# A four-layer block on one core: attention scores from fp16 halves, query and key biases as a product, projections and one value projection in other steps

## What is computed

```python
q = (x @ Wq + bq).reshape(B, S, N_HEAD, HEAD_DIM).transpose(0, 2, 1, 3)
k = (x @ Wk + bk).reshape(B, S, N_HEAD, HEAD_DIM).transpose(0, 2, 1, 3)
v = (x @ Wv + bv).reshape(B, S, N_HEAD, HEAD_DIM).transpose(0, 2, 1, 3)
scores = jnp.einsum('bhqd,bhkd->bhqk', q / math.sqrt(HEAD_DIM), k)
scores = scores + attention_bias
scores = jnp.where(src_mask, -jnp.inf, scores.astype(jnp.float32))
probs = jax.nn.softmax(scores, axis=-1).astype(v.dtype)
ctx = jnp.einsum('bhqk,bhkd->bhqd', probs, v)
```

## Time and profile before

| | |
|---|---|
| median of 3 runs | 2546.38 us (2546.37 to 2546.72) |
| the profiled execution, its own time | 2548.05 us |
| its span, first to last instruction | 2546.2 us |
| PE, DVE, ACT, POOL busy, share of the span | 97%, 75%, 44%, 38% |
| attention pass | to about 1082 us, eight sequences |

### The profile page before, as it was taken

The page is one execution under the profiler, slowest core; times in us unless marked ns, Lnnn a source line. Parts: engine busy times, 40 slices in busy tenths (PEclk is TensorE's granted clock), DMA queues, the critical chain, the costliest instruction groups (busy, mean ns, idle before and its releaser), DMA issues.

```text
span 2546.2 us, 45850 instructions
## 1 busy us (share of the span) xinstructions
PE 2470.9 (97%) x14369; PEld 1223.5 (48%) x14456; DVE 1921.7 (75%) x3700; ACT 1127.6 (44%) x2160; POOL 978.1 (38%) x829
## 2 busy tenths in 40 slices
PE   6999999999999999999999999999999999999996
PEld 4454545455555555544444444444444444444443
DVE  7877777777778685663598688678786886886887
ACT  3676757575758575742223223233222322232331
POOL 1464646464646464410044143242341441432321
PEclk8999999999999999999999999999999999999998
DMA  6445444454544445551232142133222321421340
GB/s 221 143 152 162 150 154 160 147 166 148 158 148 156 150 150 168 163 191 42 79 112 90 61 141 89 56 120 115 83 87 91 108 91 62 141 84 58 123 169 17
DMA packets 150760, 312.29 MB, mean 123 GB/s; under 512 B 16642, under 2 KB 21762, under 8 KB 150546
## 3 DMA queue, kind: packets, MB, share of 16 engines
q1 hardware_dynamic: 141330, 293.01, 35.1%
q10 hardware_dynamic: 9216, 16.78, 1.8%
HBM read 292.75 MB, written 16.81 MB: 122 GB/s over the span
## 4 chain that ended last, share of the span: by engine, by line
PE 53%; DVE 3%; issue 1%; ACT 0%; DVEq 0%; ACTq 0%
PE ffn_bank L1469 17%; PE ffn_bank L1471 17%; PE ffn_bank L1470 17%; PE ffn_bank L1455 1%; PE ffn_bank L1533 1%; PE ffn_bank L1475 1%; DVE g2T_hi L1777 1%; DVE g2T_lo L1778 0%; DVE w_lo L1835 0%; DVE w_hi L1835 0%; PE ffn_bank L1566 0%; DVE stage L1740 0%; ACT g L1611 0%; DVE stage L1721 0%; DVE f L1829 0%
## 5 line engine op out<-in xcount | busy, mean ns | idle before, releaser
L1077 DVE CUSTOM_DVE_ANT_0 w_words<-bank,stage 128x512 f32<-128x512 f32 x512 | 323.7, 686 | 92.7 <-PE bank L688 86.7
L857 ACT ACTIVATE w_words<-w_words,nmax 128x512 f32<-128x512 f32 x512 | 363.4, 714 | 42.2 <-DVE nmax L1077 42.1
L561 POOL TENSOR_TENSOR stage<-stage,mask_add 128x1024 f32<-128x1024 f32 x128 | 272.9, 2143 | 215.3 <-DMA stage<-in_bias 197.6
L1777 DVE CAST g2T_hi<-g 128x512 f16<-128x512 f32 x256 | 179.5, 701 | 221.0 <-ACT g L1611 216.5
L711 PE MATMUL bank<-ident,w_words 128*128 128x128 f32 x2048 | 299.6, 280 | 16.2 <-DVE late L1092 4.7
L711 PEld LDWEIGHTS bank<-ident,w_words 128*128 128x128 f32 x2048 | 222.7, 140 | 175.2 <-issue 83.4
L1778 DVE TENSOR_TENSOR g2T_lo<-g,g2T_hi 128x512 f16<-128x512 f32 x256 | 243.6, 951 | 8.8
L1611 ACT ACTIVATE g<-ffn_bank,bi 128x512 f32<-128x512 f32 x128 | 88.0, 687 | 350.1 <-PE ffn_bank L1471 328.9
L843 ACT ACTIVATE late<-bank 128x512 f32<-128x512 f32 x256 | 151.0, 590 | 151.7 <-PE bank L711 151.5
L1405 POOL TENSOR_TENSOR late<-late,b 128x512 f32<-128x512 f32 x32 | 39.6, 1269 | 464.0 <-DVE f L1809 464.0
L1391 POOL TENSOR_TENSOR stage<-grid,f 128x512 f32<-128x512 f32 x84 | 138.5, 1675 | 200.2 <-DVE f L1680 75.3
(11 more groups left out here) (277 smaller groups left out, 4886.3 us busy)
## 6 DMA issues: line engine op xcount, KB each, us to landing
stage<-in_bias SPq DMA_DIRECT2D x256, 512.0 KB, 4.3
stage<-in_W_l SPq DMA_DIRECT2D x128, 512.0 KB, 3.3
grid<-in_grids SPq DMA_DIRECT2D x140, 256.0 KB, 3.6
xin<-in_x SPq DMA_DIRECT2D x32, 256.0 KB, 4.0
x_rows<-w_words ACTq DMA_DIRECT2D x32, 256.0 KB, 3.7
late<-x_rows SPq DMA_DIRECT2D x8, 1024.0 KB, 8.7
out<-stage ACTq DMA_DIRECT2D x32, 256.0 KB, 2.0
l_rows<-in_rows SPq DMA_DIRECT2D x8, 768.0 KB, 6.6
```

The source lines that it names most:

```text
L561: pool.tensor_tensor(bias[:, n % NB, :, :], bias[:, n % NB, :, :], mask_add[:, u % T, :].unsqueeze(1).to_broadcast([P, 2, S]), ALU.add).th ...
L857: act.activation(tile, tile, ACT.Exp, scale=-1.0, bias=nmax[:, u % 2, i:i + 1], accum_out=rsum[:, j, h:h + 1]).then_inc(prob_ready, 1)
L1077: dve.tensor_tensor_reduce(tiles[:, 4 * (u % NR) + i, :], bank[:, :], bias[:, half % NB, i % 2, :], -1.0, 3.0e38, ALU.add, ALU.min, nmax[: ...
L1777: link(dve.tensor_copy(gT[0][:, n % 4, :], g32[:, n % 2, :]))
```

## The change

- `q32` and `k32` become pairs of fp16 halves. ScalarE writes the high half of both `q` and `k` (activation Copy with the scale), VectorE then the low half of both (the bank times the scale, minus the high half). Before, each was one instruction of one engine.
- The scores of four heads are three rounds of four fp16 products (high by high, high by low, low by high) where there were four fp32 products.
- The biases of q and k are no longer added on the way out. GpSimdE prepares once, before the loop, a tile of two rows (high and low half of the scaled bias), and every `q` or `k` projection ends with one more product of these two rows with a tile of ones.
- The table: `v 3` moves from step 1 to step 3; `q 1`, `k 1` from steps 2, 3 to 1, 2; `q 2`, `k 2` from 6, 7 to 5, 6; `q 3`, `k 3` from 10, 11 to 9, 10. The first product with v waits for each value tile alone.

```diff
-BESIDE = {0: [("v", 2), ("xT", 0), ("xT", 1)], 1: [("v", 3), ("xT", 2), ("xT", 3)],
-          2: [("down",), ("q", 1)], 3: [("expert",), ("k", 1)], 4: [("up", 0), ("up", 1)],
-          5: [("R", 0), ("up", 2), ("up", 3)], 6: [("q", 2)], 7: [("k", 2)], 9: [("R", 1)], 10: [("q", 3)],
-          11: [("k", 3)], 13: [("R", 2)], 17: [("R", 3)]}
+BESIDE = {0: [("v", 2), ("xT", 0), ("xT", 1)], 1: [("xT", 2), ("xT", 3), ("q", 1)],
+          2: [("down",), ("k", 1)], 3: [("expert",), ("v", 3)], 4: [("up", 0), ("up", 1)],
+          5: [("R", 0), ("up", 2), ("up", 3), ("q", 2)], 6: [("k", 2)], 9: [("R", 1), ("q", 3)], 10: [("k", 3)],
+          13: [("R", 2)], 17: [("R", 3)]}
...
+            pool.tensor_scalar(b_scaled, b_raw, WS, None, ALU.mult).then_inc(b_chain, 1)
...
+            pool.memset(ones[:, :], 1.0).then_inc(b_chain, 1)
...
-                        mm = three(bank[:, :], w, x, c == 0, c == C - 1)
+                        mm = three(bank[:, :], w, x, c == 0, c == C - 1 and name == "v")
+                    if name != "v":
+                        if m == 0:
+                            pe.wait_ge(b_chain, 7)
+                        mm = pe.matmul(bank[:, :], qk_b[:, "qk".index(name), m * P:(m + 1) * P], ones[:, :].to_broadcast([2, S]), start=False, stop=True)
...
-                    for i in range(4):
-                        rows = slice(HD * i, HD * i + HD)
-                        pe.matmul(psum[i][:, :], q32[rows, g, j * P:(j + 1) * P], k32[rows, g, :],
-                                  start=i < 2, stop=True).then_inc(full[i], 1)
+                    for n, (qs, ks) in enumerate(((0, 0), (0, 1), (1, 0))):
+                        for i in range(4):
+                            rows = slice(HD * i, HD * i + HD)
+                            mm = pe.matmul(psum[i][:, :], q16[qs][rows, g, j * P:(j + 1) * P], k16[ks][rows, g, :],
+                                           start=n == 0 and i < 2, stop=n == 2)
+                            if n == 2:
+                                mm.then_inc(full[i], 1)
...
-                        pe.wait_ge(v32_ready, 1 + it * T + T)
+                    if v == 0:
+                        pe.wait_ge(v32_ready, 1 + it * T + kb + 1)
...
-                        act.activation(q32[:, m, :], bank[:, :], ACT.Identity, scale=1.0 / (WS * math.sqrt(HD)),
-                                       bias=bq[:, m:m + 1]).then_inc(q32_ready, 1)
+                        act.activation(q16[0][:, m, :], bank[:, :], ACT.Copy, scale=Q_SCALE).then_inc(q_hi, 1)
+                    elif name == "k":
+                        bank = arrived(act, it, key)
+                        act.activation(k16[0][:, m, :], bank[:, :], ACT.Copy, scale=1.0 / WS).then_inc(k_hi, 1)
...
-                            for key in beside(it, u):
+                        for key in beside(it, u):
+                            if i == (3 if key[0] in ("q", "k") else ACT_AFTER.get(u, 4)):
...
-                    if name == "k":
-                        bank = arrived(dve, it, key)
-                        dve.tensor_scalar(k32[:, m, :], bank[:, :], 1.0 / WS, bk[:, m:m + 1], ALU.mult, ALU.add)\
-                            .then_inc(k32_ready, 1)
+                    if name in ("q", "k"):
+                        bank = psum[place(it, key)[0]]
+                        pair, scale, hi, ready = {"q": (q16, Q_SCALE, q_hi, q_split), "k": (k16, 1.0 / WS, k_hi, k_split)}[name]
+                        dve.wait_ge(hi, it * C + m + 1)
+                        dve.scalar_tensor_tensor(out=pair[1][:, m, :], in0=bank[:, :], scalar=scale, in1=pair[0][:, m, :],
+                                                 op0=ALU.mult, op1=ALU.subtract).then_inc(ready, 1)
...
-                        if i == DVE_AFTER.get(u, 4):
-                            for key in beside(it, u):
+                        for key in beside(it, u):
+                            if i == (4 if key[0] in ("q", "k") else DVE_AFTER.get(u, 4)):
```

46 lines of the change are left out of this document (33 added, 13 removed).

## The result

The changed kernel takes 2599.49 us (median of 4 runs, 2593.87 to 2602.56), the kernel before 2546.55 on the same chip: a ratio of 1.0202, with a 95% interval of 1.0189 to 1.0215. It is slower by about 53 us; 24.5 were forecast. The profiled execution of the changed kernel took 2602.56 us, its span is 2600.7.

What follows compares the result with a forecast made beforehand. TensorE bounds the round (busy 126.55 of 129.42 us), VectorE close behind in some steps. Scores -38.4, biases +26.6, step 2 +14, steps 6 to 13 +26.3, other waits -4: +24.5, so 2571 us; own range 2556 to 2588, outer 2541 to 2593.

Steps and rivals of the forecast that it cites:

- GpSimdE's rows: Seven small GpSimdE instructions before the loop prepare the bias rows; TensorE waits for them once, taken as nothing.
- Scores: Each score block on TensorE takes 0.77 to 0.78 us instead of 1.08; 0.30 saved in 128 blocks, -38.4 us.
- The second rival: Two-row products cost 0.217 and GpSimdE's addition misses the cast: 2548 us, no difference; chance 0.09.
- the first: VectorE keeps up, low halves and score banks are ready in time, 40 us of waits go: 2531 us; chance 0.15.
- the third: Loads wait for their own strip, 0.2 us more a score block in 100 blocks, +20: 2591 us; chance 0.08.
- Bias products: 64 two-row products added on TensorE, 0.63 us for two starts, 0.415 each: +26.6 us.
- Step 2: Third transpose waits 2.0 us for k 1's low half, behind VectorE's part g slowed by GpSimdE's addition; seven rounds, +14 us.
- Steps 6 to 8: After k 2, TensorE waits 1.1 us for score banks that VectorE reads late; part of the +26.3 us.
- Steps 10 to 13: After k 3, TensorE waits for score banks VectorE reads late: 2.3 us, 2.5 by step 14; part of +26.3 us.
- Waits that go: Step 9's 0.55 us wait for ScalarE goes, v 3 covers some 1.1 in step 3; with new waits together -4 us.
- The new waits at q 2 and q 3: Waits of 0.1 to 0.6 us where q 2 and q 3 pass two engines, 1.0 a round; counted within the -4 us.
- the trap of step 2: The wait in step 2 before the third transpose, for a low half standing behind part g on VectorE; forecast 2.0 us.

Runs made afterwards that it cites:

- c_fix: Changed kernel with the old table, q 1 ahead of the down product, high halves of q 2, k 2, q 3, k 3 behind two exponentials: 2554.37 us.
- hi_early: v1_swap with ScalarE's high halves of q 2, k 2, q 3, k 3 behind two exponentials instead of three, plus 16 dummy products: 2564.47 us.
- v1_swap: Changed kernel without bias products (each half adds the bias from a column), k 1 ahead of the down product in step 2: 2597.50 us.
- rinv_later: Changed kernel with k 1 ahead of the down product, VectorE's reciprocal and spread copy behind the tile copies, R product behind q: 2590.90 us.
- order3: No bias products, old table, q 1 ahead of the down product; high halves, v 3 and xT earlier on ScalarE, k's low half behind three readings: 2533.99 us.
- b_spin: Changed kernel with 32 dummy products on TensorE ahead of the third transpose of step 2: 2592.23 us.
- d_newtable: Kernel before (fp32 scores, no bias products) with the changed kernel's table alone: 2598.58 us.
- c_oldtable: Changed kernel (fp16 halves, bias products) with the table of the kernel before: 2585.98 us.
- v1: Changed kernel without bias products and GpSimdE's rows; each half adds the bias from a column: 2616.35 us.
- v1_old: v1 with the table of the kernel before, q 1 ahead of the down product, k 1 ahead of the expert product in step 3: 2620.05 us.

## Why the prediction was half of it

The side was right, and so were most of the places; the size was not: 53 us where 24.5 were forecast, outside the range of 2541 to 2593. The step that failed is the price of the wait in step 2: it was counted as idle time alone, 14 us, and the stretch of half clock behind it, 11.5 us more, was not in the sum. Three smaller things were missing beside it: GpSimdE's rows (put at nothing), a wait in step 9, and one at the end of a round.

- **Scores**, -0.30 a block: 0.76 measured instead of 1.08, right. The second rival (no change) and the first (VectorE keeps up) fell with the waits, the third with the rows.
- **Bias products**, 0.63 for two starts: right as a row, and TensorE does work that time. As the price of having them it is wrong. "What the change gives or takes on TensorE's list counts in full, as long as TensorE does not begin to wait" was written down and then not used: the product and the wait of the same steps were added up as if neither covered the other. Taken out of the changed kernel the products give 0.4 us a round back, not 3.3; in a good order 1.7. The list here keeps them at their full row, since waits beside them are counted separately.
- **GpSimdE's rows**, nothing: the first scores come 4.9 us later, 0.8 of it forecast. They were placed "outside the rounds", but VectorE's chain to the first norm lies there too and ended 3.0 us later beside them; the last 1 us is not explained.
- **Step 2**, a wait of 2.0: 1.97 measured. **This is the term that was mis-sized**: the wait cost 1.64 more behind it, by the clock. 14 us were 25. (The sum had the two transposes ahead at 0.87; they take 0.97, which changes little.)
- **Steps 6 to 8**, 1.1 a round: with the products priced as rows, stretch 5 to 8 should take 25.11 - 4 x 0.30 + 2 x 0.415 = 24.7; it takes 25.7, so 1.0. Right: step 7 takes 5.18 where a bare step takes 4.24.
- **Steps 10 to 13**, 2.5: the same sum for steps 9 to 13 is 29.0, measured 32.7, so 3.8. The masks ahead of steps 12 and 13 are 2.7 of it (5.46 and 5.75 for two bare steps), as forecast. Of the other 1.0, 0.8 lie in step 9, in TensorE's wait of 1.1 at its first transpose for VectorE's copy, which was not in the sum. Its cause stays open in part: it is gone with q 3 out of step 9 (in c_fix the transpose waits 0.77, for ScalarE), and it is not shorter with earlier high halves (1.23 in hi_early, 1.19 in v1_swap), while its nearest neighbour on VectorE, moved in rinv_later, took nothing away.
- **Waits that go**, -4: mostly not found. In step 9 the wait of 0.55 for ScalarE went and the one of 1.1 for VectorE came. In step 3 the kernel before had 0.26 us a round of TensorE's waiting for v 3 to cover, not 1.1. The new waits at q 2 and q 3, 1.0 a round, did not come either, so these errors cancel in part.
- **From step 15 to the next round**: 0.6 to 0.8 more than the products make. TensorE waits twice for ScalarE's copies there, 0.48 and 0.53 a round, and much the same in c_fix and order3; why stays open.

Together: the clock 11.5, the start 4, step 9 some 6, the round's end some 5; that is most of the 28 us between the forecast and the result. Of these, only the clock is shown by an experiment that takes it away and leaves all else (b_spin).

The larger fault is in what the prediction took for the cause. It took the table as given and priced products and waits in it, and the order was most of the cost. The table without the halves costs some 34 us (d_newtable without its stops), the halves in the old table 39 (c_oldtable), both together 53: both have the trap of step 2, so the two can't be added. With that trap out and the high halves one position earlier, the halves and bias products in the old table cost 7 (c_fix), a seventh. The new table puts q 2 and q 3 into steps 5 and 9 (6.3 and 5.7 us before, 9.0 and 9.2 after) and leaves two bare steps behind k 2 and k 3. In the long ones TensorE sets the pace, in the bare ones VectorE (busy 4.63 of 5.46 us in step 11 and 5.25 of 5.76 in step 12, by windows of single steps), and neither makes up for the other; in the old table q 2, q 3 and k 3 stand in steps 6, 10 and 11, where VectorE has its statistics to do.

## What to carry to other kernels

When the engine that sets the time gets less to do, ask of each step which chain of the others then sets it, and try the order of the small steps (which position a read-out has among the exponentials) before the products: here 45 of 53 us were order. What a product taken out of one step gives back, the waits of the next steps can take (2.1 of 2.1 us here), so don't add prices of work and of waits as if they stood apart. And a wait of some 2 us on TensorE can have a slow stretch behind it, here 1.64 us in each of seven rounds.

## What the hardware showed that I had not expected

- After 1.97 us without work TensorE's granted clock fell (0.61 over 2.55 us) and the products took twice as long for some 3 us; with 32 dummy products in the gap it stayed at 1.00. The wait does not always bring that: in c_oldtable, with up to 2.07 in the same place, step 3 alternates between 9.58 and 7.94 from the second round on, and in d_newtable, with 2.5, it is long in two of seven rounds (9.42, else 7.79).
- The same loop of the second pass takes 17 to 25 us more when its code lies elsewhere (d_newtable, v1, v1_swap, v1_old): six stops of 2.1 to 2.9 us, a clock that fell behind two to four of them, and 53 or 54 more instruction packets, gone with 16 more dummy products ahead of it. The Trainium skill ("Runtime: NRT & Kernel Launch", Instruction fetch mechanics) has an instruction memory of 128 KiB for TensorE, filled in blocks of 16 KiB, with a stop at a taken branch whose target lies outside the current window of two blocks. The packets' size agrees; no run here shows that memory's size. Nor does the packet count alone tell a stop: b_spin has 56 more packets, 53 of them in the second pass, and loses nothing there. In an unchanged stretch that gets slower, look for TensorE's waits put down to "issue" and then at that queue.
- GpSimdE's arithmetic takes 2.1 to 3.7 us for 1024 columns on two partitions (a cast 1.03), no less than the 2.13 for 1024 columns on 128. Beside one of them a cast of VectorE took 1.94 instead of 0.43; beside another, at 19.8 us, the same cast took its usual 0.42.
- A column of biases as an operand costs 0.075 us on ScalarE and 0.06 on VectorE for 512 columns out of PSUM (on ScalarE together with Identity in place of Copy).
